# Conv2's image 3 by pairs of output rows, with last statistics by row parity

## The reference

```python
def _L1_conv_ref(x, w1, gamma1, beta1, w2, gamma2, beta2):
    q1 = ternary_quantize(w1)                                   # weights -1, 0, 1
    out1 = relu(batchnorm(conv3x3(x, q1), gamma1, beta1))
    q2 = ternary_quantize(w2)
    out2 = batchnorm(conv3x3(out1, q2), gamma2, beta2)          # over all 4 images
    return relu(out1 + out2)

x = x + _L1_conv_ref(_gn(x), ...)
```

## Time and profile before

| | us |
|---|---|
| three runs | 275.22, 275.20, 274.11; median 275.2 |
| the profiled execution | 274.98 |
| its span in the trace | 273.2 |
| TensorE busy in the span | 241.6 (88%) |
| VectorE busy | 214.5 (79%) |
| ScalarE busy | 172.3 (63%) |
| GpSimd busy | 168.4 (62%) |

### The profile page before, as it was taken

How to read it: one execution, slowest core, us unless ns; L and a number is a source line. 1 busy time by engine, 2 the same in 40 slices (tenths; PEclk the granted TensorE clock), 3 DMA queues, 4 the chain that set the end, 5 groups by cost and what they waited for, 6 DMA issues and landing times.

```text
span 273.2 us, 5575 instructions
## 1 busy us (share of the span) xinstructions
PE 241.6 (88%) x1944; PEld 209.2 (77%) x1944; DVE 214.5 (79%) x472; ACT 172.3 (63%) x364; POOL 168.4 (62%) x218
## 2 busy tenths in 40 slices
PE   2599998999989999998998999989999999999800
PEld 2487667799988789987998898989987776777600
DVE  5689555989897999559987779986488797699493
ACT  2478765979777978877789877857316406640140
POOL 8210499999767868786686996574910600937051
PEclk9999998899999999999999999999999999999965
DMA  7924777543443322333322333310000000000016
GB/s 216 374 68 150 222 258 240 164 151 124 135 140 126 126 96 75 108 117 108 106 98 86 107 124 126 104 45 0 2 0 0 2 1 0 0 0 2 5 50 262
DMA packets 25593, 28.13 MB, mean 103 GB/s; under 512 B 2509, under 2 KB 23613, under 8 KB 25560
## 3 DMA queue, kind: packets, MB, share of 16 engines
q1 hardware_dynamic: 24912, 25.95, 28.9%
q10 hardware_dynamic: 648, 1.76, 1.8%
HBM read 19.87 MB, written 6.78 MB: 98 GB/s over the span
## 4 chain that ended last, share of the span: by engine, by line
PE 59%; DVE 21%; ACT 9%; issue 4%; DMA 3%; POOL 1%; SPq 1%; POOLq 0%; DVEq 0%
PE PS L940 13%; PE PS L847 6%; PE PS L800 5%; PE PS L849 5%; PE PS L848 5%; PE PS L829 4%; DVE slo L1548 4%; PE PS L975 4%; PE PS L831 4%; PE PS L830 4%; DVE vlo L1559 3%; ACT vhi L1156 3%; PE PS L729 3%; DVE st L1447 2%; ACT shi L1144 2%
## 5 line engine op out<-in xcount | busy, mean ns | idle before, releaser
L583 POOL TENSOR_TENSOR vt<-rowm,hat 128x1026 f32<-128x1026 f32 x36 | 70.8, 1967 | 26.7 <-PE PS L809 25.2
L1559 DVE TENSOR_TENSOR vlo<-PS,vhi 128x576 fp32r<-128x576 f32 (+2 forms) x88 | 50.0, 588 | 18.1 <-ACT vhi L1156 17.8
L1156 ACT ACTIVATE vhi<-PS 128x576 fp32r<-128x576 f32 (+2 forms) x88 | 43.8, 523 | 19.6 <-PE PS L831 19.4
L1548 DVE TENSOR_TENSOR slo<-PS,shi 114x512 fp32r<-114x512 f32 (+1 forms) x68 | 43.2, 673 | 6.4 <-ACT shi L1144 6.1
L847 PE MATMUL PS<-vhi,wdhi 128*128 128x256 f32 x144 | 43.5, 302 | 1.1 <-ACT xb L1163 1.1
L829 PE MATMUL PS<-shi,patch 114*128 114x288 f32 (+1 forms) x136 | 43.2, 318 | 0.5 <-DVE omr L1822 0.3
L830 PE MATMUL PS<-slo,patch 114*128 114x288 f32 (+1 forms) x136 | 40.8, 300 | 0.0
L831 PE MATMUL PS<-shi,patch 114*128 114x288 f32 (+1 forms) x136 | 40.6, 298 | 0.0
L848 PE MATMUL PS<-vlo,wdhi 128*128 128x256 f32 x144 | 40.5, 281 | 0.0
L849 PE MATMUL PS<-vhi,wdlo 128*128 128x256 f32 x144 | 40.5, 281 | 0.0
L1144 ACT ACTIVATE shi<-PS 114x512 fp32r<-114x512 f32 (+1 forms) x68 | 36.7, 592 | 4.3 <-PE PS L800 3.7
(11 more groups left out here) (214 smaller groups left out, 513.1 us busy)
## 6 DMA issues: line engine op xcount, KB each, us to landing
patch<-xt SPq DMA_DIRECT2D x136, 114.0 KB
xt<-xtv SPq DMA_DIRECT2D x4, 1024.0 KB, 6.3
xs<-in_x SPq DMA_DIRECT2D x3, 512.0 KB, 7.9
wraw<-in_L_conv_w SPq DMA_DIRECT2D x2, 576.0 KB, 9.8
out<-xb SPq DMA_DIRECT2D x4, 256.0 KB, 2.6
wd_raw<-in_L_conv_weight ACTq DMA_DIRECT2D x1, 576.0 KB, 7.1
xs<-in_x SPq DMA_DIRECT2D x2, 256.0 KB, 4.0
omr<-omr SPq DMA_DIRECT2D x8, 64.0 KB, 4.4
```

Source lines behind the costliest of these rows:

```text
L583: g.tensor_tensor(vt[:, n % 2, :, :].rearrange("p t (r j) -> p t r j", r=WR), rowm[:, n % 2, :, :].unsqueeze(3).to_broadcast([P, TAPS, WR, ...
L1156: last = a.activation(places(vhi), src, ACT.Copy)
L1548: d.tensor_tensor(lo, src, hi, ALU.subtract).then_inc(slo_ok, 1 if pairs(n) == 2 else 3)
L1559: last = d.tensor_tensor(places(vlo), src, places(vhi), ALU.subtract)
```

## The change

Image 3 of Conv2 becomes a point image too, w = 4 (`ALL` = 5 of them in all), and its direct convolution is dropped. Its planes take `vfs`, after the tails of w = 2 (`wl_ok`), its parts take `xtv`, its points the banks 4 to 7, and its output stands in PSUM banks 4 and 5. The high and low parts of r1's image 3 in `xhi` and `xlo` (ScalarE L1266, VectorE L1729) are no longer made. The output of w = 3 goes to `xb` instead of PSUM, and ScalarE copies it into banks 6 and 7 when the last ends are done (`back_ok` 2), which VectorE's last passes wait for.

In the orders: VectorE gets the sum of w = 4 between the tails of w = 3 and the sums of w = 2, its tails after the statistics of image 1, its sums, ends and statistics at the end, the latter by row parity, each behind its half of the ends. GpSimd makes the differences of w = 4 straight after those of w = 3, and its additions to r1 wait for all tails. ScalarE makes the copy of w = 2 before the heads of w = 3, and the copy of w = 3 before the heads of w = 4. TensorE does p0 with both parts before p3 in w = 4.

```diff
--- before.py
+++ after.py
@@ -348,12 +348,14 @@
 
 
         NW = B - 2
-        W_BANKS = [dict(zip((1, 2, 0, 3), m)) for m in ((3, 4, 5, 6), (0, 1, 2, 3), (2, 3, 4, 5), (6, 7, 2, 3))]
+        ALL = NW + B - 1
+        POOL_SUMS = ()
+        W_BANKS = [dict(zip((1, 2, 0, 3), m)) for m in ((3, 4, 5, 6), (0, 1, 2, 3), (2, 3, 4, 5), (6, 7, 2, 3), (4, 5, 6, 7))]
         C1_BANKS = ((0, 1), None, None, (6, 7))
         C2_BANKS = ((0, 1), (2, 3), (6, 7), (4, 5))
 
         def image_of(w):
-            return w % NW + 1
+            return w + 1 if w < NW else w - NW + 1
 
         def plane(w):
 
@@ -385,7 +387,7 @@
             return m[:, H:2 * H, kx:kx + W].rearrange("p (t e) x -> p t e x", e=2)[:, :, (0, 1)[p == 3], :]
 
         def point_weight(w, p, kx):
-            return (q1, q2)[w // NW][:, kx, :] if p == 0 else qg[w // NW][:, p - 1, kx, :]
+            return (q1, q2)[w >= NW][:, kx, :] if p == 0 else qg[w >= NW][:, p - 1, kx, :]
 
         def pair_rows(m, e):
 
@@ -395,7 +397,7 @@
 
             if w < NW:
                 return pair_rows(r1[:, image_of(w), :], e)
-            if w == NW:
+            if w < ALL - 1:
                 return pair_rows(xb[:, image_of(w), :], e)
             return pair_rows(conv2_out(image_of(w)).rearrange("p a x -> p (a x)"), e)
 
@@ -606,7 +608,7 @@
                 b = image_of(w)
                 m = plane_rows(w)
                 if w >= NW:
-                    pool.wait_ge(wl_ok, 2 * NW)
+                    pool.wait_ge(wl_ok, 2 * NW + 2 * (w == ALL - 1))
                     pool.wait_ge(xlo_ok, 4)
                     pool.wait_ge(r1_ok, b + 1)
                 else:
@@ -654,11 +656,14 @@
             point_weights(1)
 
             pool.wait_ge(vpad, 4)
-            for w in range(NW, 2 * NW):
-                point_differences(w)
-            pool.wait_ge(wl_ok, 4 * NW)
+            point_differences(NW)
+            point_differences(NW + 1)
+            point_differences(NW + 2)
+            pool.wait_ge(wl_ok, 2 * ALL)
             for n in range(POOL_CHUNKS, 2 * B):
-                pool.wait_ge(*((wv_dif, 4 * NW) if n // 2 == 2 else (r1lo_ok, 3)))
+                w = NW + n // 2 - 1
+                pool.wait_ge(wv_sum, w + 1)
+                pool.wait_ge(wv_dif, 2 * w + 2)
                 g.tensor_tensor(chunk(r1, n), chunk(r1, n), chunk(xs, n), ALU.add).then_inc(r1x_ok, 1)
             for n in range(POOL_CHUNKS):
                 pool.wait_ge(f_relu, n + 1)
@@ -926,12 +931,9 @@
                 if done is c1_mm:
                     pe.wait_ge(xhi_ok, B + b // 3 + 1) if part == 0 else pe.wait_ge(xlo_ok, 2 + b // 3 + 1)
                 else:
-                    pe.wait_ge((r1hi_ok, r1lo_ok)[part], 3 if b else 1 if (h, part) == (0, 0) else 2)
+                    pe.wait_ge((r1hi_ok, r1lo_ok)[part], 1 if (h, part) == (0, 0) else 2)
                 if b and not part:
-                    if done is c1_mm:
-                        pe.wait_ge(*((gn_var, order(GN1, B - 1) + 1) if h else (wy_ok, 2)))
-                    else:
-                        pe.wait_ge(wy_ok, 2 * NW + h + 1)
+                    pe.wait_ge(*((gn_var, order(GN1, B - 1) + 1) if h else (wy_ok, 2)))
                 bank = (C1_BANKS if done is c1_mm else C2_BANKS)[b][h]
                 for i, k in enumerate(TAP_ORDER[part]):
                     if done is c2_mm and (b, h, part, k) == (0, 0, 0, 2 * K):
@@ -955,19 +957,21 @@
                     pe.wait_ge(wc_ok, 1)
                 elif w == 3 and p in (1, 2):
                     pe.wait_ge(r1_ok, 4)
-                    pe.wait_ge(r1hi_ok, 3)
-                elif w == 3 and p == 0:
-                    pe.wait_ge(wc_ok, 3)
-                elif w == 3:
-                    pe.wait_ge(ws_ok, 6)
+                elif w == 4 and p in (1, 2):
+                    pe.wait_ge(wy_ok, 4 + p)
+                elif w >= 3:
+                    pe.wait_ge(*((ws_ok, 2 * w) if p else (wc_ok, w)))
 
             def conv_points(w, sums=()):
 
-                pe.wait_ge(qg_ok, 4 * (w // NW) + 4)
+                pe.wait_ge(qg_ok, 4 * (w >= NW) + 4)
                 pe.wait_ge(vpad, 1 + w % NW)
                 done = 0
                 for m, points in enumerate(POINTS):
-                    for p, part in [(p, part) for part in range(2) for p in points]:
+                    steps = [(p, part) for part in range(2) for p in points]
+                    if w == ALL - 1 and m:
+                        steps = [(p, part) for p in points for part in range(2)]
+                    for p, part in steps:
                         pe.wait_ge((wh_ok, wl_ok)[part], 2 * w + m + 1)
                         if part == 0:
                             bank_free(w, p)
@@ -998,11 +1002,8 @@
                 for part in range(2):
                     for h in range(2):
                         conv_part(q2, 0, h, part, c2_mm)
-                for w in range(NW, 2 * NW):
+                for w in range(NW, ALL):
                     conv_points(w)
-                for part in range(2):
-                    for h in range(2):
-                        conv_part(q2, 3, h, part, c2_mm)
 
             slot(-2)
             turn_offsets(2)
@@ -1194,7 +1195,8 @@
                 act.wait_ge(w_mm, 4 * w + 2)
                 if w:
                     act.wait_ge(ws_ok, 2 * w)
-                a.activation(wcopy[:, 0:BIG], PS[:, W_BANKS[w][1], :], ACT.Copy).then_inc(wc_ok, 1)
+                m, n = W_BANKS[w][1], 2 if w in POOL_SUMS else 1
+                a.activation(wcopy[:, 0:n * BIG], PS[:, m:m + n, :].rearrange("p a x -> p (a x)"), ACT.Copy).then_inc(wc_ok, 1)
 
             def beside(n):
                 for b in range(B - 1):
@@ -1263,13 +1265,17 @@
                     point_heads(NW, m)
                 last_out = PS[:, C1_BANKS[3][0]:C1_BANKS[3][1] + 1, :].rearrange("p a x -> p (a x)")
                 rectify(r1[:, 3, :], last_out).then_inc(r1_ok, 1)
-                rectify(inner(xhi, 3), square(last_out)).then_inc(r1hi_ok, 1)
+                point_copy(NW)
                 for m in range(2):
                     point_heads(NW + 1, m)
-                point_copy(NW)
                 point_copy(NW + 1)
-                act.wait_ge(wy_ok, 4 * NW)
+                for m in range(2):
+                    point_heads(NW + 2, m)
+                act.wait_ge(wy_ok, 2 * NW + 4)
                 a.activation(conv2_out(1).rearrange("p a x -> p (a x)"), plain(1), ACT.Copy).then_inc(back_ok, 1)
+                point_copy(NW + 2)
+                act.wait_ge(wy_ok, 2 * ALL)
+                a.activation(conv2_out(2).rearrange("p a x -> p (a x)"), plain(2), ACT.Copy).then_inc(back_ok, 1)
                 root(BN2, 0)
                 act.wait_ge(gn_ok, order(BN2, 0) + 1)
                 for n in range(POOL_CHUNKS):
@@ -1578,7 +1584,7 @@
                     d.scalar_tensor_tensor(out=out, in0=pair_rows(m, 0), scalar=twice, in1=pair_rows(m, 1),
                                            op0=ALU.add, op1=ALU.add).then_inc(wv_sum, 1)
                 else:
-                    dve.wait_ge(wl_ok, 2 * NW)
+                    dve.wait_ge(wl_ok, 2 * NW + 2 * (w == ALL - 1))
                     dve.wait_ge(xlo_ok, 4)
                     dve.wait_ge(r1_ok, b + 1)
                     d.tensor_tensor(out, pair_rows(m, 0), pair_rows(m, 1), ALU.add).then_inc(wv_sum, 1)
@@ -1721,24 +1727,26 @@
                     conv_stats(BN2, h, PS[:, h, :])
                 for m in range(2):
                     point_tails(NW + 1, m)
+                point_sum(NW + 2)
                 point_sums(NW)
                 for e in range(2):
                     point_ends(NW, e)
-                dve.wait_ge(r1_ok, 4)
-                dve.wait_ge(r1hi_ok, 3)
-                d.tensor_tensor(inner(xlo, 3), square(r1[:, 3, :]), inner(xhi, 3), ALU.subtract).then_inc(r1lo_ok, 1)
                 for h in range(2):
                     dve.wait_ge(wy_ok, 2 * NW + 2)
                     conv_stats(BN2, 2 + h, ychunk(2 + h))
+                for m in range(2):
+                    point_tails(NW + 2, m)
                 point_sums(NW + 1)
                 for e in range(2):
                     point_ends(NW + 1, e)
                 for h in range(2):
-                    dve.wait_ge(wy_ok, 4 * NW)
-                    conv_stats(BN2, 4 + h, PS[:, C2_BANKS[2][h], :])
-                for h in range(2):
-                    dve.wait_ge(c2_mm, 3 + h)
-                    ins = conv_stats(BN2, 6 + h, PS[:, C2_BANKS[3][h], :])
+                    dve.wait_ge(wy_ok, 2 * NW + 4)
+                    conv_stats(BN2, 4 + h, ychunk(4 + h))
+                point_sums(NW + 2)
+                for e in range(2):
+                    point_ends(NW + 2, e)
+                    dve.wait_ge(wy_ok, 2 * NW + 5 + e)
+                    ins = conv_stats(BN2, 6 + e, pair_rows(conv2_out(3).rearrange("p a x -> p (a x)"), e))
                 link(ins)
                 whole_stats(BN2)
                 variance(BN2, 0)
```

(1 more changed line is left out.)

## The result

The changed kernel took 277.95 us in the median of four runs (277.36 to 280.30) against 275.21 for the kernel before. The ratio is 1.0114 with a 95% interval of [1.0078, 1.0150], so between 2.1 and 4.1 us slower, 3.1 in the middle. Its profiled execution took 277.83 us with a span of 276.0, against 274.98 and 273.2.

The account below looks back on a forecast made before the run. TensorE bounds Conv2 before, VectorE after the change: VectorE's excess work, its waits and GpSimd's 2.2 us block bring the aggregate 3.4 us later; 274.98 + 3.4 = 278.4 us, range 276.0 to 280.4.

Parts of the forecast that it names:

- The forecast case: In Conv2, VectorE becomes the bound and GpSimd blocks its tails: aggregate +3.4 us, 278.4 us in all; chance 0.64.
- What bounds it: End of Conv2: TensorE bounds the kernel before, with 2.7 us on offer; VectorE, idle only 3.53 us, becomes the bound.
- VectorE's excess: VectorE in Conv2: 4.1 us more work, 0.35 copy wait, 0.3 own-result waits, less 3.53 idle: +1.2 us.
- The block: At 243.3 us, GpSimd's 128x1024 difference of w=4 meets VectorE's tails of w=3: VectorE loses 2.2 us, bounds 0 to 3.5.
- the two orders that I left open: At 243.3 us, GpSimd's difference or VectorE's first tail of w=3 goes first; either way VectorE loses 2.2 us.
- the sharing: Tails beside GpSimd's differences: reading their slower mean as shared bandwidth gives 1.9 us, against 2.2 to 2.4 for full blocking.
- Rival (c): At 241.58 us GpSimd goes first again though VectorE has waited since 239.25: +1.3 us more, 279.7 us; chance 0.08.
- a wait until 249.8: TensorE at p3 of w=3, reached at 247.5 us, waits for `ws_ok` until 249.8; costs nothing, 3.2 us to spare.
- Rival (d): TensorE's clock falls to 1.2 GHz in its gap near 248 us: +5 us, 283.4 us at most; chance 0.08.
- a gap of 2.3 us: TensorE's longest forecast gap, at p3 of w=3; split in two (1.5 and 0.7) if GpSimd is first at 243.3.
- the one before 10.47: TensorE's gap of 2.22 us before 10.47 in the profile, which left its clock full.
- rival (a): GpSimd's differences and VectorE's tails miss each other, no block: +1.2 us, 276.2 us; chance 0.13, 0.16 with slips.

Follow-up runs that it names:

- e3: Kernel before, with 12 of the 36 matmuls of image 3's direct convolution in Conv2 left out: stretch 29.95 us, ratio 0.9884.
- e4: Changed kernel, with 10 matmuls of 512 columns added ahead of p1 of w=4: stretch 36.11 us, ratio 1.0148.
- e10: Kernel before, with the two statistics of Conv2's image 1 reading 32 columns each instead of 512: stretch 32.82 us, ratio 0.9992.
- e8: Changed kernel, with the two statistics of Conv2's image 1 reading 32 columns each instead of 512: stretch 35.39 us, ratio 1.0081.
- e1: Changed kernel, with GpSimd's second difference of w=4 waiting for the tails of w=3 and the sum of w=4: stretch 33.93 us, ratio 1.0054.
- e6: Changed kernel, GpSimd's second w=4 difference after the sum of w=4, ScalarE's w=4 copy ahead of image 1's: stretch 33.56 us, ratio 1.0029.
- e9: e7 with the sum of w=4 moved from VectorE to GpSimd: stretch 31.94 us, ratio to the kernel before 0.9976.
- e7: Changed kernel, same work reordered on VectorE, ScalarE and GpSimd: stretch 31.99 us in both runs, ratios to the kernel before 0.9979 and 0.9982.

## Why the prediction was right

Forecast 278.4 us, range 276.0 to 280.4; measured 277.95. The forecast case is the one that came, and its steps can be checked one by one, so the number wasn't right by luck.

- **What bounds it.** TensorE before, VectorE after: right. e3 takes 2.86 us by 12 matmuls fewer before, e4 costs nothing with 10 more after; e10 and e8 say the same of VectorE's load, the other way round.
- **VectorE's excess.** Forecast +1.2 us with no block, of which 0.35 is the wait for ScalarE's copy. e1 measured +1.12, and without the wait e6 +0.75. Two small terms were off: no row shows the 0.62 us of the sum of w=4 (the sum of w=3 stood blocked), it took 0.60; and the tails' 2.36 is busy time, from start to start two cost 2.28, and 2.26 in w=4.
- **The block.** Forecast +2.2 us; e1 took 2.20 away. Of the two orders that I left open, GpSimd's came: it started 0.08 us ahead. In the trace of after the first tail waited for the rest of one whole GpSimd instruction. The Trainium skill's page "SBUF — State Buffer", section "Who interferes with whom", says that the later instruction blocks fully. The trace agrees: 3.40 us for the blocked tail. If the two had shared at half speed, it would have been done in some 2.4 us (an estimate from the 1.21 us that it takes alone) and GpSimd's instruction would have been slowed, which kept its 2.40. By the sharing my sum would have been 0.3 us too low.
- **GpSimd's order at 241.** Rival (c), that it goes first again while VectorE's sum waits, did not come: its 128x512 difference took 1.74 us, 0.45 of it behind the sum.
- **TensorE.** Forecast a wait until 249.8 at p3 of w=3, w=4 at 252.1 and the end at 258.1; measured, with the run's offset of 0.43 added, 249.8, 252.15 and 258.3. The gap came split, 1.30 and 0.55 us (forecast 1.5 and 0.7 for this order; from start to start 1.55 and 0.72).
- **The clock.** Rival (d) did not come: 1.00 granted from 245 to 250. But its 2.6 us from the last matmul to the fall were one case of many: it is 2.1 us in the profile of after (257.8 to 260.0), 2.4 in e3, 4.5 in e1 and 5.1 in e9. So a gap of 2.3 us in one piece, the longest that I allowed for, was not shown to be safe; and the one before 10.47 tells little, since the same trace has the clock at 1.00 through its first 4.21 us too, in which there is no matmul at all.
- **The end.** ScalarE's wait 0.29 for 0.35; the second copy back (1.03 us from 261.52) is over 0.11 us ahead of the root at 262.66. The adds of GpSimd start at 254.10 and are far from being waited for. Closing steps 13.75 for 13.84 us.
- **The sum.** Stretch +3.32 for +3.4. On top, the median came 0.45 us lower than the forecast. The profile of after itself started Conv2 0.43 us earlier than that of before, which no step of mine could tell.

What I had too rough was outside the sum: how well rival (a), 0.44% above before, can be told from no change. With the four runs of the result it can't, since the interval of their ratio is 0.7% wide; the block on top made the result clear. With eleven runs it can: e1, which is the kernel of rival (a), has an interval of 1.0035 to 1.0074.

## What to carry to other kernels

Before an engine is relieved by giving work to its neighbours, count the idle time that the neighbour has left in exactly that stretch: here 3.5 us for 4.1 us of work, which already ate the gain of 2.9. Two engines that exclude each other (here VectorE and GpSimd when both read both of their inputs from SBUF) are one queue, and an instruction "in free time" of the one has to be placed where the other works from PSUM; one wait more gained 2.2 us of the stretch, and an order that uses the gaps turned +3.3 into -0.8.

## What the runs showed of the hardware

The same instructions ahead of Conv2 took between 225.85 and 227.25 us up to the aggregate of Conv1's batch norm in the profiles of these kernels, a scatter of 1.4 us. The stretch between the aggregates was 31.99 us in both profiles of e7 (the only kernel profiled twice), and e10 and e4, whose edits cost it nothing, lie 0.01 and 0.02 us from before and after. Effects under 1 us are better read from a stretch than from the time of the kernel.

Of VectorE and GpSimd, the one that is first keeps its time, and the second pays. GpSimd's 128x1024 difference takes 2.40 us beside a blocked tail (before and after) and 2.39 us where VectorE reads PSUM (e1); its 128x512 one, which takes 1.29 us alone, takes 1.74 behind VectorE's sum of w=3 (after), where it is the second. VectorE's sum of w=2, 0.04 us ahead of GpSimd, keeps its 0.69 us, and the GpSimd instruction beside it takes 1.80 (after, 231.4 us). With both queues full they take turns: between the two tails of w=2 stands GpSimd's 128x512 difference, 2.27 us long since the waiting tail goes ahead of it, and the second tail then waits for it.
